# Retention and mixture of experts on one core: state sums moved directly behind the scores, k's and q's projections side by side, and the scores as eight tiles of 32 by 64

## The reference, cut to what matters

```python
x = layernorm(x)
q, k, v = x @ W_q.T, x @ W_k.T, x @ W_v.T            # as 16 heads of 16
decay[h, i, j] = gamma[h] ** (i - j) if i >= j else 0
attn = einsum('bihd,bjhd->bhij', q, k) * decay / sqrt(16)
y = einsum('bhij,bjhd->bihd', attn, v)
y = (y - mean(y over time and head)) / sqrt(var + eps) * gn_weight + gn_bias
x1 = x_in + y @ W_o.T
out = x1 + (shared(layernorm(x1)) + experts(layernorm(x1)) / 2) / 2
```

## Time and profile before

| | |
|---|---|
| time, median of 3 runs | 445.52 us (444.48 to 446.04) |
| the profiled execution: time / span | 445.83 us / 444.0 us |
| PE busy | 436.3 us (98%) |
| weight loads busy | 391.8 us (88%) |
| DVE, ACT, POOL busy | 296.7, 216.9, 95.6 us |
| granted TensorE clock | 1.0 |

### The profile page before, as it was taken

How to read it: one execution, slowest core, us unless ns; L and a number is a source line. 1 busy time by engine, 2 the same in 40 slices (tenths; PEclk the granted TensorE clock), 3 DMA queues, 4 the chain that set the end, 5 groups by cost and what they waited for, 6 DMA issues and landing times.

```text
span 444.0 us, 14549 instructions
## 1 busy us (share of the span) xinstructions
PE 436.3 (98%) x6318; PEld 391.8 (88%) x6318; DVE 296.7 (67%) x685; ACT 216.9 (49%) x416; POOL 95.6 (22%) x73
## 2 busy tenths in 40 slices
PE   6999999999999999999999999999999999999997
PEld 5999998999999999998989988899988999888995
DVE  6887788766877778876656663857548575575433
ACT  3565556545773567535246342472424723346430
POOL 1103223522245023550531100311004020040000
PEclk9999999999999999999999999999999999999999
DMA  7543332222341121325240014100123001120011
GB/s 260 157 133 98 99 98 75 75 68 80 122 121 52 51 97 51 99 98 185 101 142 1 0 50 173 65 0 0 47 98 138 0 0 47 47 94 0 1 47 47
DMA packets 15382, 34.64 MB, mean 78 GB/s; under 512 B 2368, under 2 KB 2656, under 8 KB 14816
## 3 DMA queue, kind: packets, MB, share of 16 engines
q1 hardware_dynamic: 14896, 33.05, 22.5%
q10 hardware_dynamic: 432, 0.79, 0.6%
HBM read 25.44 MB, written 8.40 MB: 76 GB/s over the span
## 4 chain that ended last, share of the span: by engine, by line
PE 96%; DMA 2%; DVE 1%; ACT 0%; issue 0%; ACTq 0%; POOL 0%; DVEq 0%
PE bank L358 52%; PE bank L367 13%; PE bank L437 7%; PE bank L368 7%; PE bank L475 4%; PE bank L466 4%; PE bank L451 3%; PE bank L416 2%; DMA wqkv_raw<-wattn 2%; PE bank L554 2%; PE bank L377 1%; PE bank L491 1%; ACT keo L687 0%; PE bank L481 0%; PE bank L485 0%
## 5 line engine op out<-in xcount | busy, mean ns | idle before, releaser
L770 ACT ACTIVATE xres<-bank,r1b 128x256 f32<-128x256 f32 x64 | 26.8, 470 | 54.9 <-PE bank L368 53.6
L358 PE MATMUL bank<-x2hi,sw_hi 128*128 128x512 f32 x128 | 51.3, 400 | 0.0
L358 PE MATMUL bank<-x2lo,sw_hi 128*128 128x512 f32 x128 | 50.4, 394 | 0.0
L755 ACT ACTIVATE sil<-bank,s1b 128x512 f32<-128x512 f32 x32 | 22.0, 688 | 58.1 <-PE bank L358 58.1
L358 PE MATMUL bank<-x2hi,sw_lo 128*128 128x512 f32 x128 | 50.3, 393 | 0.0
L367 PE MATMUL bank<-sw_both,ghi 128*128 128x512 f32 x128 | 46.5, 396 | 0.0
L367 PE MATMUL bank<-w_both,ehi 128*128 128x512 f32 x128 | 46.4, 397 | 0.0
L865 DVE TENSOR_TENSOR pm<-bank,msk 128x512 f32<-128x512 f32 x64 | 39.8, 683 | 9.2 <-PE bank L437 9.2
L1037 DVE SCALAR_TENSOR_TENSOR gf<-bank,s3b,sil 128x512 f32<-128x512 f32 x32 | 23.9, 748 | 32.1 <-PE bank L358 32.1
L687 ACT ACTIVATE keo<-kT,msk 128x512 f32<-128x512 f32 x32 | 21.4, 714 | 39.6 <-DVE kT L854 39.6
L358 PE MATMUL bank<-xhi,wqkv_hi 128*128 128x256 f32 x128 | 39.3, 307 | 0.6 <-DVE xlo L849 0.5
(11 more groups left out here) (119 smaller groups left out, 1133.1 us busy)
## 6 DMA issues: line engine op xcount, KB each, us to landing
xin<-xa SPq DMA_DIRECT2D x16, 256.0 KB, 3.1
w_raw<-w SPq DMA_DIRECT2D x16, 256.0 KB, 3.1
xres<-xs SPq DMA_DIRECT2D x16, 256.0 KB, 3.3
x_scratch<-xres SPq DMA_DIRECT2D x16, 256.0 KB, 3.1
xl<-x_scratch SPq DMA_DIRECT2D x8, 512.0 KB, 5.2
xr<-x_scratch SPq DMA_DIRECT2D x4, 1024.0 KB, 4.9
out<-xr SPq DMA_DIRECT2D x7, 512.0 KB, 2.6
sw_raw<-sw SPq DMA_DIRECT2D x6, 256.0 KB, 3.6
```

What stands on the lines that cost most here:

```text
L358: mm = nc.tensor.matmul(o, w[c][l], x[c][r], start=first and c == 0 and j == 0, stop=last and c == n - 1 and j == 2)
L755: nc.scalar.activation(sil[i % 2][:], h1_bank[i % 2][:], ACT.Silu, bias=s1b[:, m:m + 1]).then_inc(sil_ready, 1)
L770: ge = nc.scalar.activation(hf[q % 2][:, m, :], e_bank[q % 4][:, m * 2 * P:(m + 1) * 2 * P], ACT.Gelu, bias=r1b[:, e, m:m + 1])
```

## The change

In `scores`, each product with 128 weight columns becomes two with 64, one for the even and one for the odd head. The array then holds eight tiles of 32 rows by 64 columns, and a part has 64 products in place of 32. All four pairs of one parity come first, then the four of the other.

On PE, `state_sums(h)` moves ahead of `project_k(h + 1)` for parts 1 to 14, so that it stands directly behind `scores(h)`, and `project_k` and `project_q` follow each other. `from_scores(h)` stands directly behind `from_state(h)` in every part, ahead of `head_vars` and `output_bias`. On ACT, `copy_v(h + 1)` moves ahead of `high_x(h + 2)`. Nothing else changes.

```diff
@@ scores
-                        for p in range(PAIRS):
-                            at = slice(32 * p, 32 * p + 32)
-                            mm = nc.tensor.matmul(p_bank[p][:, o:o + CH], keo[at, c, g, :, :],
-                                                  qT[h % 2][at, g, c * CH:(c + 1) * CH], start=True, stop=True)
+                        for odd in range(2):
+                            for p in range(PAIRS):
+                                at = slice(32 * p, 32 * p + 32)
+                                mm = nc.tensor.matmul(p_bank[p][CH * odd:CH * odd + CH, o:o + CH], keo[at, c, g, odd, :],
+                                                      qT[h % 2][at, g, c * CH:(c + 1) * CH], start=True, stop=True)
@@ step of PE
-                if h + 1 < PARTS:
+                if h == 0:
+                    project_k(1)
+                state_sums(h)
+                if 0 < h < PARTS - 1:
                     project_k(h + 1)
-                state_sums(h)
@@
-                if b and s >= 2 and h + 1 < PARTS:
-                    from_scores(h)
+                from_scores(h)
                 if b and s == 0:
                     head_vars(b - 1, p_bank[0])
@@
-                if not (b and s >= 2) or h + 1 == PARTS:
-                    from_scores(h)
@@ step of ACT
                 if h + 1 < PARTS:
                     copy_k(h + 1)
+                    copy_v(h + 1)
                 if h + 2 < PARTS:
                     high_x(h + 2)
-                if h + 1 < PARTS:
-                    copy_v(h + 1)
```

## The result

The changed kernel takes 471.3 us (467.8 to 477.4, 6 runs) against 445.2 us of the kernel before in the same rounds: a ratio of 1.0575 (95% interval 1.0531 to 1.062). It is 26 us slower, where 6.5 us less were forecast. One of the six executions, the one of 477.4 us, fell in a slower state of the chip and is left out of the ratio. The profiled execution took 469.3 us with a span of 467.5.

The account below looks back on a forecast made before the run. PE was taken as the bound. 14 steps of 0.47 us, plus smaller gains and losses, made 6.4 us; following every wait gave 6.5, so 439.1 us, with a range of 436 to 443.5.

Parts of the forecast that it names:

- What bounds the kernel: Whole kernel: PE has work in 98% of the span, so time taken from its blocks comes back one for one.
- The scores in eight tiles: Scores block on PE: eight tiles work at once, 1.03 to 1.33 us in place of 1.94; 1.03 taken.
- each record keeps its price of 30 ns: Scores block: 3.88 us a block, some 470 us in all; chance 0.08 together with the slower rival of 452 us.
- Fewer changes of the tiling: State sums behind scores, project_k and project_q together: one turn of the tiling saved a part, 0.2 us.
- The new wait: Plain retention step: PE waits 0.4 us for low_x before project_k, so the step gains 0.47 us, not 1.1.
- Only the order helps: Rival, scores block: four tiles at a time, load hidden, 2.06 us; no wait for low_x; 443.0 us; chance 0.07.
- from_scores ahead of the small products: Around head_vars and output_bias: six places gain 1.2 us; late copy_bias on ACT costs 1.2 us.
- The state's late arrival: Parts 5, 9, 13: gn_affine on DVE between low_x and masks makes from_state wait about 0.3 us, three times, 0.9.
- Signs: Profile after: scores 1.0 to 1.3 us, project_k waiting about 0.4 us for low_x, state sums 0.2 for v's copy.

Follow-up runs that it names:

- the burst: The kernel before with 512 products of zeros in eight tiles of 32 by 64 put into its warm-up: 472.5 us in one run.
- the shift: The changed kernel with 32 small products of zeros (128 instructions) added to the warm-up: 460.8 us, 1.0306 to the kernel before.
- The order alone: The changed kernel with the scores as before (32 products of 32 by 128 a part), all of the new order kept: 444.2 us, 0.9945 to the kernel before.

## Why the prediction was wrong

*What bounds the kernel* holds the step that failed. "What is taken from PE's blocks comes back one for one, as long as no other engine is late" leaves out the supply of PE's own instructions: the sum puts it at nothing, and it cost 20.7 us of idle time on PE. The forecast counted the 128 records that the new scores block brings, and never what it takes to bring their instructions. The kernel before had the warning: a hole of 0.38 us called "issue" within part 5's from_state, and 0.5 us in that line of the earlier trace rows. It lies at number 193 plus a multiple of 256 as well. I took it for noise.

*The scores in eight tiles* is the term through which it failed. The forecast took 1.03 us and held 1.33 for the upper bound of eight tiles at once. Eight tiles do work at once, at 9 ns a record. But the block takes 1.52 us by the chain, since only the first 32 pairs of load and matmul go at that pace and the rest at 11 ns. By the text's own reasoning that would have changed nothing, for anything under some 1.6 us disappears into the wait for low_x; no run without holes has tested it. What it cost is that 256 instructions in 1.5 us, and 384 in 2.35 with the state sums behind, outrun a supply of 256 in 3.46 us (shown by the burst, by the shift and by the numbers of the holes). No rival named this, and the range hadn't room for it. The rival "each record keeps its price of 30 ns", at 470 us, is near the measured time by chance: its mechanism, a scores block of 3.9 us, isn't there.

*The size of the loss.* Idle time with no releaser on PE is 15.0 us in the state sums, 2.5 in scores, 2.0 before projections and 1.2 in from_scores: 20.7 us, where the kernel before had 0.5. Five stretches at the lower clock come to some 5 to 7 us, an estimate from the 1.5 us that the two projections at 105.24 took beyond 3.07. PE's matmuls wait 1.2 us for low_x (0.5 before), 0.8 for v's copy and 0.6 for k's. 0.4 us a part of shorter scores and 0.2 of turns go off, 9 us. Together that is some 18 to 20, where the profiled span grew by 23.5. State sums with a hole in them also take longer beside it, 0.42 + 0.62 us around the hole at 102.5 where the whole block was 0.83; if each of the 15 holes costs these 0.2 us, that is 3 more, an estimate again. What is left isn't laid to anything.

*Fewer changes of the tiling*: right, 0.2 us a part (3.07 for k and q together in place of 3.25).

*The new wait*: right in kind, and hardly tested. It was to come in nearly every part, 0.4 us for low_x and 0.2 for v's copy; PE's matmuls in the changed kernel wait for each of them in three parts only. In the others a hole seems to have given ACT and DVE the time, which isn't shown part by part. The variant with ACT's old order shows a wait for v's copy at 0.27 us a part. The order alone was put at 4.3 us (the 2.5 of the rival *Only the order helps*, with its 0.12 a part for the scores taken out again) and measured 2.5 by the ratio; where the rest went is open. The variant shows waits for low_x and the state in single parts only, as forecast.

*from_scores ahead of the small products*: 1.0 us less measured, inside its bounds. *The state's late arrival* was there three times in the new order with the old scores, 0.2 us in place of 0.3.

*Signs.* I had written that I'd be wrong if project_k started without waiting, for then the scores would be slow. In most parts it did start without waiting, but the scores block is 1.52 us and not slow. Nothing listed was a hole inside a block that waits for nothing.

## What to carry to other kernels

Splitting products into more and smaller tiles buys array time with instructions, and here each 256 of PE's instructions cost 3.46 us in a run that stayed dense, even where the array did them in 1.6. Count loads and matmuls of each run of tiled products, and compare 256 of them with that period before counting what the array saves. How much of the excess is paid depends on what stands around it; by the runs here, a slow block between two dense ones (projections, 24 instructions in 1.5 us) looks like cover, which an order that puts dense blocks side by side takes away. Nearly the same program gained 10 us by where the packets ended in it, so a small change far ahead of a dense block can move the time for no reason of its own. To see it in a profile, number PE's instructions and look whether the idle time without a releaser always falls on the same number modulo 256.

## What the runs showed of the hardware

- PE's instructions come in packets of 16 KB, 256 instructions, and in a dense run a packet passes each 3.46 us: about 1.1 until its transfer starts, 0.9 to 1.0 of transfer, 1.4 from landing to first use (the burst, at the full and at half of the clock). Under other traffic the start came up to 3.4 us after the boundary. Behind a slower block it came with the boundary, and two boundaries were passed within 2.2 us.
- Eight tiles of 32 by 64 start at 9 ns a record over the first 32 records of a block, and at 11 ns over the rest; four tiles of 128 by 32 start at 16 ns.
- Behind or at the end of five holes the granted clock fell to half. PE's matmuls had been idle for 1.7, 2.0, 2.1, 2.4 and 3.9 us in them; behind one of 2.05 us it didn't fall. The two projections behind one of the five took 4.56 us in place of 3.07.
- A turn from the full array to a tiled form and back costs 0.2 us (k and q: 3.25 us with a tiled block between them, 3.07 without).
